# Attention and FFN layer on eight cores: the next head pair's Q/K projection moves into the steps of the current pair's attention

## The reference, cut to what matters

```python
def reference(x, Wq, bq, Wk, bk, Wv, bv, Wo, bo, G1_R, G2_R, G1_I, G2_I, bias_real, bias_imag):
    # x: (8, 2048, 1024), 16 heads of 64
    h = layernorm(x)
    Q, K, V = (split_heads(h @ W + b) for W, b in ((Wq, bq), (Wk, bk), (Wv, bv)))
    scores = einsum('bhnd,bhmd->bhnm', Q, K) / sqrt(64)
    scores = scores + power_law_mask(2048, 0.25)      # -0.25*log(i-j), -inf above the diagonal
    x = x + merge_heads(softmax(scores) @ V) @ Wo + bo
    h = layernorm(x)
    W_real, W_imag = unfold_tt(G1_R, G2_R), unfold_tt(G1_I, G2_I)     # 512 x 512 each
    re, im = split(h, 2)
    out = concat(re @ W_real.T - im @ W_imag.T + bias_real,
                 re @ W_imag.T + im @ W_real.T + bias_imag)
    return x + out
```

## Time and profile before

| | us |
|---|---|
| median of 3 runs | 1401.54 |
| lowest and highest run | 1398.28, 1421.76 |
| profiled execution | 1408.81 |
| its span on the slowest core, 7 | 1407.3 |
| spans of the eight cores | 1384.0 to 1407.3 |
| mean granted TensorE clock of the cores | 0.706 to 0.726 |

### The profile page before, as it was taken

How to read it: one execution, slowest core, us unless ns; L and a number is a source line. 1 busy time by engine, 2 the same in 40 slices (tenths; PEclk the granted TensorE clock), 3 DMA queues, 4 the chain that set the end, 5 groups by cost and what they waited for, 6 DMA issues and landing times.

```text
span 1407.3 us, 13883 instructions; the slowest of 8 cores (1384.0 to 1407.3 us)
## 1 busy us (share of the span) xinstructions
PE 869.2 (62%) x3672; PEld 269.9 (19%) x3672; DVE 602.3 (43%) x1163; ACT 467.0 (33%) x891; POOL 165.3 (12%) x128
## 2 busy tenths in 40 slices
PE   0101477777577587676775666786756566565566
PEld 0000223212112112112122112112111222222222
DVE  4545332543543543543443653443441634433432
ACT  0101100375473563573662663662750000000000
POOL 2221200101201101201003340000000201101100
PEclk9999978768558557568567557557666677776767
DMA  4111503100202102102002200000022110111101
GB/s 96 51 54 60 75 1 45 61 16 8 68 1 30 46 0 31 46 0 52 24 1 60 90 31 1 1 1 0 1 52 53 45 60 0 60 60 60 60 31 60
DMA packets 39394, 52.52 MB, mean 37 GB/s; under 512 B 21782, under 2 KB 23830, under 8 KB 39192
## 3 DMA queue, kind: packets, MB, share of 16 engines
q1 hardware_dynamic: 18520, 43.25, 9.4%
q0 software_dynamic: 20800, 8.39, 4.9%
HBM read 51.63 MB, written 8.39 MB: 43 GB/s over the span
## 4 chain that ended last, share of the span: by engine, by line
PE 44%; DVE 21%; issue 11%; ACT 10%; DMA 8%; DVEq 3%; POOL 2%; ACTq 0%; SPq 0%; POOLq 0%
PE stP L370 9%; ACT PTb L594 7%; DMA xrot<-x 7%; PE psF L889 6%; PE pv L642 6%; PE stP L569 5%; DVE PTb L618 5%; PE stP L458 4%; DVE PTb L613 4%; PE pr L657 4%; PE psW L822 3%; DVE stat L217 3%; POOL sqscr L215 2%; DVE cmS L404 2%; DVE stat L231 2%
## 5 line engine op out<-in xcount | busy, mean ns | idle before, releaser
L594 ACT ACTIVATE PTb<-stP,negCS 128x512 bf16<-128x512 f32 (+1 forms) x320 | 199.0, 622 | 258.0 <-PE stP L575 257.2
L642 PE MATMUL pv<-PTb,V 128*64 128x512 bf16 (+1 forms) x320 | 164.3, 513 | 162.6 <-DVE PTb L618 160.2
L613 DVE TENSOR_TENSOR PTb<-PTb,decayS 128x512 bf16<-128x512 bf16 (+1 forms) x320 | 143.1, 447 | 262.8 <-ACT PTb L594 261.2
L599 ACT ACTIVATE PTb<-stP,negCS 128x512 bf16<-128x512 f32 (+1 forms) x320 | 197.1, 616 | 0.0
L650 PE MATMUL pv<-PTb,V 128*64 128x512 bf16 (+1 forms) x320 | 172.5, 539 | 0.0
L663 PE MATMUL pr<-PTb,ones 128*64 128x512 bf16 (+1 forms) x320 | 171.3, 535 | 0.0
L657 PE MATMUL pr<-PTb,ones 128*64 128x512 bf16 (+1 forms) x320 | 171.2, 535 | 0.0
L569 PE MATMUL stP<-QTs,KTs 64*128 64x512 bf16 (+1 forms) x320 | 164.2, 518 | 4.6 <-ACT negCS L428 3.7
L575 PE MATMUL stP<-QTs,KTs 64*128 64x512 bf16 (+1 forms) x320 | 164.8, 520 | 0.0
L239 ACT ACTIVATE stat<-stat 128x1 f32<-128x1 f32 x32 | 6.5, 203 | 431.8 <-DVEq L234 431.8
L618 DVE TENSOR_TENSOR PTb<-PTb,decayS 128x512 bf16<-128x512 bf16 (+1 forms) x320 | 139.6, 436 | 18.2 <-ACT PTb L599 0.8
(11 more groups left out here) (90 smaller groups left out, 1021.5 us busy)
## 6 DMA issues: line engine op xcount, KB each, us to landing
xrot<-x SPq DMA_DIRECT2D x32, 512.0 KB, 4.3
g1b<-g1rep SPq DMA_DIRECT2D x32, 256.0 KB, 2.7
g2b<-g2rep SPq DMA_DIRECT2D x32, 256.0 KB, 3.0
out<-outbuf SPq DMA_DIRECT2D x8, 1024.0 KB, 4.9
Wqp<-wq POOLq DMA_DIRECT2D x8, 256.0 KB, 4.8
Wkp<-wk POOLq DMA_DIRECT2D x8, 256.0 KB, 5.6
WvS<-wv POOLq DMA_DIRECT2D x2, 1024.0 KB, 10.3
WoS<-wo POOLq DMA_DIRECT2D x1, 2048.0 KB, 15.4
```

Of the source, the lines that this page charges most:

```text
L594: s.activation(PTb[:, slot * 1024 + no:slot * 1024 + 512], stP[j][:, no:512], AF.Exp, bias=negCS[:, pi:pi + 1]),
L599: s.activation(PTb[:, slot * 1024 + 512 + no:(slot + 1) * 1024], stP[j][:, 512 + no:1024], AF.Exp, bias=negCS[:, pi:pi + 1]),
L613: P.emit("vector", lambda v, slot=slot, off=off, no=no: v.tensor_mul(PTb[:, slot * 1024 + no:slot * 1024 + 512], PTb[:, slot * 1024 + no:s ...
L642: t.matmul(pv[cpi][0:64, no:512], V[:, mt * 1024 + h0 * 64:mt * 1024 + h0 * 64 + 64], PTb[:, slot * 1024 + no:slot * 1024 + 512], start=(m ...
```

## The change

The Q/K work of pair p + 1 is turned into a generator. emit_qk_compute gets a yield after each of its pieces: each of the 8 chunks, each square, each pair of norm matmul and reduction, and each link of the small chain. A new gen_pair_filler(p) strings together the weight DMAs of pair p + 2, the pieces of pair p + 1 and now five W-build units. In each step of pair p, behind the scores, exps and multiplies, the next piece is emitted. So step 0 takes the weight DMAs, steps 1 to 8 one projection chunk each, steps 9 and 14 a square, steps 10 to 13 and 15 to 18 a norm matmul with its reduction, steps 19 to 22 the small chain, and steps 22 to 27 the W-build units (units go to SP and POOL alone). After the 40 steps nothing is left over, and the next pair's scores follow directly.

To have PSUM for it, the pool of the projection gets two banks of its own (qk0, qk1), and pv and pr go from two banks to one each. So the first attention-V of every chunk waits for the second multiply out of pv of the chunk before. The reciprocal and the multiplies are the same operations (QUARTER_NORM is off). Pair 0's projection and V still stand ahead of attention, on the new banks.

```diff
-        pool = PsumPool(stP)
+        qkP = [pscope.enter_context(nc.psum_tensor("qk0", [128, 512], F32)),
+               pscope.enter_context(nc.psum_tensor("qk1", [128, 512], F32))]
+        pool = PsumPool(qkP)
...
                     pool.release(j, aE, er)
+                    yield
...
                 sq = P.emit("vector", lambda v: v.drain(fusable=False), inc=vE)
+                yield
...
                     pool.release(j, vE, red)
+                    yield
...
-            return ng
+            negc[p] = ng
...
-            pv = [AVS.enter_context(nc.psum_tensor("pv0", [128, 512], F32)),
-                  AVS.enter_context(nc.psum_tensor("pv1", [128, 512], F32))]
-            pr = [AVS.enter_context(nc.psum_tensor("pr0", [128, 512], F32)),
-                  AVS.enter_context(nc.psum_tensor("pr1", [128, 512], F32))]
-            pvpr_free = [None, None]
+            pv = AVS.enter_context(nc.psum_tensor("pv0", [128, 512], F32))
+            pr = AVS.enter_context(nc.psum_tensor("pr0", [128, 512], F32))
+            aev_q = [None, None, None, None]
+            pvpr_free = None
             aev_last = 0
+
+            def gen_pair_filler(p):
+                if p + 2 < PAIRS:
+                    emit_qk_weights(p + 2)
+                yield
+                if p + 1 < PAIRS:
+                    yield from emit_qk_compute(p + 1)
+                for _ in range(5):
+                    emit_wbuild_unit()
+                    yield
...
-                        if pvpr_free[cpi] is not None:
-                            wv_.append(pvpr_free[cpi])
+                        if pvpr_free is not None:
+                            wv_.append(pvpr_free)
...
+                filler = gen_pair_filler(p)
                 for k in range(S):
                     if k >= 2:
                         emit_attnV(k - 2)
                     emit_ST(k)
                     emit_exp(k)
                     emit_mult(k)
+                    if INTERLEAVE_QK:
+                        next(filler, None)
                 emit_attnV(S - 2)
                 emit_attnV(S - 1)
+                for _ in filler:
+                    pass
                 gstep = g0 + S
-                pool.free_req[0] = (aE, exp_by_j[0]) if exp_by_j[0] else None
-                pool.free_req[1] = (aE, exp_by_j[1]) if exp_by_j[1] else None
                 qkslot_gate[pi] = (tE, gav[gstep - 1])
-                if p + 2 < PAIRS:
-                    emit_qk_weights(p + 2)
-                if p + 1 < PAIRS:
-                    negc[p + 1] = emit_qk_compute(p + 1)
...
-                for _ in range(4):
-                    emit_wbuild_unit()
```

More of the change, by code:

```diff
@@ L64 @@
 PARANOID = False
+INTERLEAVE_QK = True
+QUARTER_NORM = False
 def build_program():
@@ L423, in emit_qk_compute @@
             cb = P.emit("vector", lambda v: v.drain(fusable=False), inc=vE)
+            yield
             j, pw = pool.acquire()
             rm = P.emit("tensor", lambda t, j=j: t.matmul(
-                stP[j][:, 0:1], hselTS[:, :], cmbf[:, :], start=True, stop=True),
+                qkP[j][:, 0:1], hselTS[:, :], cmbf[:, :], start=True, stop=True),
                 waits=[(vE, cb)] + pw, inc=tE)
             ng = P.emit("scalar", lambda s, j=j, pi=pi: s.activation(
-                negCS[:, pi:pi + 1], stP[j][:, 0:1], AF.Copy, scale=-0.5),
+                negCS[:, pi:pi + 1], qkP[j][:, 0:1], AF.Copy, scale=-0.5),
                 waits=[(tE, rm)], inc=aE)
             pool.release(j, aE, ng)
-            return ng
+            negc[p] = ng
+            if DEBUG_TAPS and p == PAIRS - 1:
+                P.emit("gpsimd", lambda g: g.dma_start(
+                    out=taps["t_qt"], in_=QTs[:, :]),
+                    waits=[(aE, ng)], inc=dG, k=16)
+                P.emit("gpsimd", lambda g: g.dma_start(
+                    out=taps["t_kt"], in_=KTs[:, :]), inc=dG, k=16)
+                P.emit("gpsimd", lambda g: g.dma_start(
+                    out=taps["t_negc"], in_=negCS[:, :]), inc=dG, k=16)
         emit_qk_weights(0)
@@ L436, in build_program @@
         negc = [None] * PAIRS
-        negc[0] = emit_qk_compute(0)
+        for _ in emit_qk_compute(0):
+            pass
         v_done = 0
@@ L457, in build_program @@
                         P.emit("tensor", lambda t, j=j, mt=mt, half=half, tin=tin:
[L458 removed]
+                               t.matmul(qkP[j][:, 0:512],
                                         ftv(xnT)[:, tin, mt * 128:(mt + 1) * 128],
@@ L670, in emit_attnV @@
                     gav[g0 + k] = tE.v
[L671 to L683 removed]
+                    if (QUARTER_NORM and mt >= 4 * c) or \
+                       (not QUARTER_NORM and islast):
+                        if QUARTER_NORM:
+                            q = mt - 4 * c
+                            lo, wd = 128 * q, 128
+                        else:
+                            q = 3
+                            lo, wd = 0, 512
+                        h = wd // 2
@@ new lines, in emit_attnV @@
+                        rb = P.emit("scalar", lambda s, lo=lo, h=h: s.activation(
+                            recipS[:, lo + h:lo + 2 * h],
+                            recipS[:, lo + h:lo + 2 * h],
+                            AF.Exp, scale=-1.0), inc=aE)
+                        base = p * SEQ + c * 512 + lo
+                        P.emit("vector", lambda v, lo=lo, base=base, h=h: v.tensor_mul(
+                            attn_outT[:, base:base + h],
+                            pv[:, lo:lo + h], recipS[:, lo:lo + h]),
+                            waits=[(aE, ra)])
@@ new lines, in emit_attnV @@
+                        ae_ = P.emit("vector", lambda v, lo=lo, base=base, h=h: v.tensor_mul(
+                            attn_outT[:, base + h:base + 2 * h],
+                            pv[:, lo + h:lo + 2 * h], recipS[:, lo + h:lo + 2 * h]),
+                            waits=[(aE, rb)], inc=vE)
+                        aev_q[q] = (vE, ae_)
+                        aev_last = ae_
+                        if q == 3:
+                            pvpr_free = (vE, ae_)
+                    if islast and DEBUG_TAPS and p == PAIRS - 1 and c == 0:
+                        d1 = P.emit("vector", lambda v: v.tensor_copy(
+                            sqscr[:, 0:512], pv[:, :]),
+                            waits=[(tE, gav[g0 + k])], inc=vE)
+                        d2 = P.emit("vector", lambda v: v.tensor_copy(
+                            sqscr[:, 512:1024], pr[:, :]),
+                            waits=[(vE, d1)], inc=vE)
+                        pvpr_free = (vE, d2)
+                        P.emit("sync", lambda s: s.dma_start(
+                            out=taps["t_pvpr"], in_=sqscr[:, :]),
+                            waits=[(vE, d2)], inc=dS, k=16)
+                        P.emit("gpsimd", lambda g: g.dma_start(
+                            out=taps["t_v"], in_=V[:, :]), inc=dG, k=16)
```

84 lines of the change are left out of this document (26 added, 58 removed).

## The result

The changed kernel takes **1287.2 us** (median of 10 runs, 1280.2 to 1297.0) beside 1399.5 for the kernel before on the same chip: ratio 0.920 with a 95% interval of 0.917 to 0.923. The profiled execution has a span of 1285.0 us on core 5, the slowest; the spans of the cores are 1261.0 to 1285.0, their granted clocks 0.771 to 0.794, where they were 0.706 to 0.726. Some runs fall into a slower state of the chip whatever the kernel, so each ratio in this document takes the other runs alone, and since the chips differ too, a difference between two kernels that ran on different chips is the difference of their ratios times 1400 us, good to some 10 us.

The account below looks back on a forecast made before the run. Attention was taken as latency-bound at 1.2 GHz with PE nearly full, and gaps between pairs as idle for exps. Terms summed to -8.6 us a pair, -60 for seven, +2 in pair 7: 1344 us, range 1300 to 1390.

Parts of the forecast that it names:

- gap: Between head pairs: the stretch without exps, near 30.7 us, shrinks to 3.1, removing 27.6 us a pair.
- steps 1-8, projection: Steps 1 to 8: 64 projection matmuls, mostly at full clock, make 24.1 us of 16.6, adding 7.5 a pair.
- steps 9-18, squares and norms: Steps 9 to 18: two exposed squares (3.2 us) and eight norm matmuls (2.4) add 5.6 a pair.
- steps 19-22, chain: Steps 19 to 22: the small dependent operations, each with a step to finish in, add 1.5 us a pair.
- steps 23-38 (forecast: single bank, +1.4): Chunk ends: attention-V waits for the multiply out of the one pv bank, 0.7 us twice, 1.4 a pair.
- POOL: Weight build, now all beside attention, slows DVE's decay multiplies: 3 us more a pair.
- The first one to two steps fall at the lower clock: Steps 1 and 2: PE starts the projection at 1.2 GHz, so they take 4.0 and 3.7 us.
- The first rival: Steps 1 to 8: PE stays at 1.2 GHz, 1436 us in all; chance 0.10 together with no overlap.
- the case without overlap: Steps 9 to 22: PE waits as long as in the gap's last 14 us, 1440 us; counted in the 0.10.
- 0.3 per step: Steps 9 to 18: a norm matmul and tile switch at 1.2 GHz lengthen each of eight steps by 0.3 us.
- the third rival: Beyond step 8: PE stays at full clock for 21 more steps, saving 6 us a pair, 1302 us; chance 0.13.
- The wait for the square: Steps 9 to 18: a PE matmul waits for the square on DVE and two hops, 1.6 us exposed, twice a pair.

Follow-up runs that it names:

- the two kernels with 8 units: Kernel before and changed kernel, each with 24 of the 32 W-build units left out: 1384.5 us (ratio 0.988) and 1253.2 us (0.895).
- e3: Changed kernel with only weight DMAs and projection chunks inside the steps; norms, small chain and W-build units behind step 39: 1371.0 us, ratio 0.978.
- e5: Changed kernel with each projection chunk cut into two pieces of four matmuls, filling steps 1 to 16: 1272.2 us, ratio 0.907.
- e10: Changed kernel with half projection chunks, first norm matmuls one step later behind their squares, and W-build units held until the small chain is through: ratio 0.880.
- e8: Changed kernel with an empty piece behind each square, so its first norm matmul comes one step later: 1276.4 us, ratio 0.909.
- e1: Changed kernel with the interleaving off, so one pv/pr bank but Q/K work again behind the 40 steps: 1414.4 us, ratio 1.009.

## Why the prediction was wrong in size

Point by point in the prediction's own terms, per pair. The stage terms are measured from the two kernels with 8 units, so that they are free of POOL but for the first pairs, where those units run, and POOL's is the difference of 4.7 (84.5 - 79.8) and 2.8 (101.3 - 98.5).

| term | forecast | measured |
|---|---|---|
| gap | -27.6 | -27.9 |
| steps 1-8, projection | +7.5 | +5.8 |
| steps 9-18, squares and norms | +5.6 | +3.8 |
| steps 19-22, chain | +1.5 | +0.6 |
| steps 23-38 (forecast: single bank, +1.4) | +1.4 | -1.1 |
| POOL | +3 | +1.9 |
| sum | -8.6 | -16.9 |

The sum is off by 8.3 us a pair, and 5.2 of them lie from step 9 on: 1.8 in the norms, 0.9 in the chain, 2.5 in steps 23 to 38. The projection has 1.7, POOL 1.1, the gap 0.3. All terms that add time are too large, and a sum of small remainders behind a gain of 27.6 shows every one of them, seven times over. (Of the two chunk ends that the 1.4 prices, one falls at step 14, in the row above it.)

*The gap* was right: 3.0 us stay where 3.1 was read off.

*The projection*: the steps at full clock were right to 0.2 us. In pair 2 steps 3 to 8 take 16.2 us (20.77 less 4.56 for steps 1 and 2), forecast 16.4. **The step that failed is "The first one to two steps fall at the lower clock"**, priced at 4.0 + 3.7; they took 4.6. The eight slow matmuls start beside the reciprocals, in the 3 us already counted as what stays of the gap, and the second group already ran at full clock (1.90 for eight). Against that, the base of 16.6 us from the earlier trace rows held POOL work and is 15.1 without it, an error of 1.5 the other way. The first rival (half clock, 1436) is out, with 0.98 and 0.99 in these steps on average, and so is the case without overlap (1440), since norms and chain went from 14 us of their own to 4.2 inside the steps.

*The norms*: **the step that failed is the half clock assumed from step 9 on**, in "0.3 per step" and in the 1.5 for the chain, and the argument that pair 6 of the kernel before "stayed at 0.50". On average over pairs and cores steps 9 to 18 ran at 0.69, 19 to 22 at 0.81, and 23 to 38, where the forecast gave nothing back, at 0.65; with 8 units it was 0.72, 0.95 and 0.74. The argument on pair 6 rested on one core: its seven others had 0.57 to 0.63 in that pair, and pair 1 stood at 0.60 in the earlier trace rows itself, so half clock was not even the rule for attention alone. What came is the third rival, in part: it had 6 us a pair for 21 steps at full clock, and steps 23 to 38 gave 1.1 on average without POOL and 3.1 at most (pair 6, slowest cores). Its price also rested on unlike steps, as the scores in the earlier trace rows are 384 columns wide and those in the earlier trace rows 512. I gave it 0.13. Pair 4 was the longest, as said (90.7 us on core 5 by the starts of its exps). That the extra PE work goes with the higher clock is seen from two sides: taking the norms out (e3) lets the clock of steps 19 to 22 fall from 0.81 to 0.57, so that they gain only 0.2 us, and spreading the dense work over more steps (e5, e10) carries 0.9 or more further down the pair.

The Trainium skill, TensorE: Matmul & The Clock Gate, part 1, has activity release the throttle. The trace agrees that the denser stretches hold full clock (1.00 in steps 1 to 8 of pair 6). The engine's busy share in the profile is no guide to it, however: 0.50 with PE busy for 14.16 of 17.90 us, 0.91 with 15.73 of 25.61, in part because each matmul takes longer at the lower clock.

*The wait for the square* was costed at 1.6. The waits read above are 3.82 us beside POOL and 2.42 without it, and PE waited 47.0 in 16 times, at most 5.3. This part was too small, though the whole term for steps 9 to 18 was too large. The prediction named as a sign of being wrong a wait of several us ahead of each norm matmul; it came ahead of the first one behind each square and not of the others. In e8 and e10 the waits are 10.8 and 13.2 in all.

*The single bank* cost 12 us by itself (e1), as forecast, though PE's wait at a chunk's end is 1.8 on average (42.8 over 24) and not under 1 as said; the 0.95 of the prediction is 0.83 by its own rows (408.41 - 407.58). *POOL* cost 1.9 a pair by the exps' starts and 2.7 by the times, at most the forecast's 3. The Trainium skill, GPSIMD Engine Reference, section Specifications, speaks of contention for DVE operations with two SBUF inputs. Groups by line of the changed kernel agree:

```profile
L410 DVE TENSOR_REDUCE cmS<-qk 2x1 f32<-2x512 f32 x64 | 42.8, 673 | 3.4 <-PE qk L405 2.6 <-PE pr L690 0.2
...
L397 DVE TENSOR_TENSOR qsqT<-QTs 128x2048 bf16<-128x2048 bf16 x8 | 10.8, 1349 | 15.9 <-ACT KTs L385 15.9
```

The reductions out of PSUM keep 673 ns against 675 in the earlier trace rows, now with POOL beside many of them (0.67 at 460.33, among POOL's casts); the squares go from 1226 to 1349, and a decay multiply beside POOL takes 1.41 (456.40).

What stays open: how much of the 4 us in steps 9 to 18 is the two stalls and how much the norm matmuls, as the runs change both together; and why one core keeps 0.50 through steps 23 to 38 and another 0.91 in the same pair of the same kernel.

## What to carry to other kernels

A chain of small dependent operations that stands alone (14 us here) shrinks to 4 once each link has an attention step to finish in, and gained more here than the large matmuls that stood beside it. Price moved work at both clock levels when it changes how dense PE is, and look at the stages behind it too: the time that it gives back there is part of the sum. In queues that run in order, put what PE waits for two steps ahead (15 us here), fill each step only up to the next engine's bound (18), and keep a third engine's contention away from the links that PE waits for (nothing alone, 23 with both others).
